# Full-width PSUM evacuation of key and query units in the first attention, 512-byte placement transfers, and a new order of projections

## The chip, the cores and the metric

The kernel runs on one core of a Trainium2 chip. The metric is device microseconds of the whole kernel. Engines are named as in the profile: PE is TensorE, ACT is ScalarE, DVE is VectorE, POOL is GpSimd, SP is SyncE, which here only issues DMA transfers.

## The reference

A decoder of two layers over x of shape (8, 128, 128): per layer a self-attention, a cross-attention and a feed-forward part, each followed by a residual sum and a layer norm. The change touches the first self-attention alone:

```python
x = _layernorm(x + _L0_attn_ref(x, wq, wk, wv, wo))      # first of six such lines
...
xq = jnp.einsum('bsh,oh->bso', x, wq)                    # wq, wk, wv: (1024, 128)
xk = jnp.einsum('bsh,oh->bso', x, wk)
xv = jnp.einsum('bsh,oh->bso', x, wv)
xq = xq.reshape(bsz, 16, seqlen, 64)                     # a reshape, not a transpose
...
scores = softmax(jnp.einsum('bhid,bhjd->bhij', xq, xk) * 64 ** -0.5)
out = jnp.einsum('bhij,bhjd->bhid', scores, xv)
```

Since the reshape does not transpose, a head is made of eight tokens, and each token gives sixteen rows of 64 numbers to it. So what a projection puts out has to be laid out anew before a head's scores can be computed.

## The kernel before, in words

**Pairs, quads, ticks.** The eight batches are worked on as four pairs (256 tokens each, p = 0 to 3). A pair has 32 heads, and four heads make a quad, so a pair has 8 quads (QP) and the attention 32 (NQ). The main loop has one tick for each quad t. In tick t PE computes the key-side scores of quad t (`scores_k`, L574 to L576), then the values of quad t - 1 (`weigh`, L592), then the query-side scores of quad t + 5 (`scores_q`, L560 and L561), which DVE reduces to row maxima (`maxima`, L1101). So the first query-side scores of pair 1, quad 8, are due in tick 3, those of pair 2 in tick 11 and those of pair 3 in tick 19.

**Projections.** A pair's projections are twelve units: 0 to 3 keys, 4 to 7 queries, 8 to 11 values. Pair 0's are done before the ticks, at eight PSUM banks; those of pairs 1 to 3 between the other work, in up to three places of a tick, at two banks in turn (`projected_at`), so that a unit waits until the bank of the last unit but one is free (`pj_free`). A table `PJ` gave the units of each tick: 3, 2, 2, 2, 1, 1, 1, 0 and again from the start for the next pair.

**Emptying a unit.** The scores are computed with float16 halves: ACT writes the upper half of a key or query unit (`empty_projection`, L899), DVE subtracts it from PSUM and writes the lower half (`lower_parts`, L1096). Both write straight into the layout that the matmuls read, in two instructions of 64 partitions, since partitions 0 to 63 and 64 to 127 of a unit belong to different columns of it. The upper half goes to partitions 0 to 63 and the lower to 64 to 127 of `KA` (keys) or `QS` (queries). `KB` is `KA` with its halves swapped, and two transfers of 64 partitions by 8 KB (SP, L330 and L332) make it. `KA`, `KB` and `QS` exist twice, for even and odd pairs.

**SP's queue.** SP issues in program order, and each wait holds back all that is behind it: all loads of inputs first; then for each pair p the two `KB` transfers, two stores of values to DRAM (L335), and, once these have landed, sixteen loads of them into `V` (L342). `scores_q` waits for `qk_in`, which these `KB` transfers raise. The order is written by hand.

**Other names of the change.** `w_abs` (L1362, L1364, L849, L1368): sums of the last feed-forward's weights, in ticks 0 to 2. `VE`: buffers of the second attention's values, which POOL sets to zero early (L431). Groups of batches in the later stages ("mid", "late") start in tick 14.

## Time and profile before

| | us |
|---|---|
| median of 3 runs (lowest to highest) | 331.54 (330.96 to 332.50) |
| the profiled execution's own time | 331.54 |
| its span in the profile | 329.7 |
| PE busy, share of the span | 253.7, 77% |
| DVE busy | 209.2, 63% |
| ACT busy | 147.6, 45% |

The profile is of one execution. Times are microseconds from the start of the span. A matmul's end is modelled, so a busy PE is not a PE at its peak; PEclk is the share of TensorE's full clock that was granted. DMA share is the mean busy share of the 16 DMA engines. In a timeline row the bracket gives how long the engine had been idle and what released it.

### The profile page before, as it was taken

Reading aid. Unit: us, or ns where it says so; the run is one execution under the profiler, and the core shown is the slowest. Engines: PE = TensorE matmul, PEld = TensorE weight load, DVE = VectorE, ACT = ScalarE, POOL = GpSimd, SP = SyncE. Lnnn points to the kernel's source line nnn. Section 1 sums busy time; section 2 is a strip of 40 time slices with the busy share of each in tenths; the row PEclk is TensorE's granted clock in tenths of the full one; section 3 lists DMA queues with packets and bytes.
Section 4 is the critical chain, followed back from the end, with each engine's and each line's share of the span. In section 5 each row is a group of like instructions: output and inputs, shape, how many; then the busy total and the mean of one; then the engine's idle time right before and its main releaser. Section 6 shows DMA issues by size and latency. Waiting matters only on the chain.

```text
span 329.7 us, 6843 instructions
## 1 busy us (share of the span) xinstructions
PE 253.7 (77%) x2658; PEld 191.9 (58%) x2658; DVE 209.2 (63%) x534; ACT 147.6 (45%) x275; POOL 72.1 (22%) x107
## 2 busy tenths in 40 slices
PE   3578679989998999798967999999887767652430
PEld 3546667978787988686844666666564434240110
DVE  2855996499657995765544666567475756354662
ACT  5962663376339545425322444453344543202651
POOL 5793000000011001443017473252020002021002
PEclk9967999999999999999978999999999896555555
DMA  7994631543142503444000800013000000000011
GB/s 233 393 258 141 139 67 66 137 104 82 67 129 64 129 34 118 103 115 51 2 1 2 155 2 2 2 40 66 3 0 2 1 2 0 0 0 1 0 32 32
DMA packets 27823, 22.86 MB, mean 69 GB/s; under 512 B 19152, under 2 KB 24400, under 8 KB 27088
## 3 DMA queue, kind: packets, MB, share of 16 engines
q1 hardware_dynamic: 27792, 22.43, 25.9%
q8 instruction: 21, 0.34, 0.5%
q14 instruction: 10, 0.08, 0.1%
HBM read 12.20 MB, written 6.03 MB: 55 GB/s over the span
## 4 chain that ended last, share of the span: by engine, by line
PE 47%; DVE 26%; ACT 13%; issue 8%; POOL 3%; DMA 1%; SPq 1%; ACTq 0%; DVEq 0%; POOLq 0%
DVE arena L1096 6%; ACT arena L899 4%; PE PS L516 4%; PE PS L619 3%; PE PS L696 3%; ACT xt L922 3%; PE PS L592 3%; PE PS L718 2%; PE PS L560 2%; PE PS L611 2%; PE PS L702 2%; PE PS L701 2%; PE PS L561 2%; POOL rstd L443 2%; DVE stats L1155 2%
## 5 line engine op out<-in xcount | busy, mean ns | idle before, releaser
L441 POOL TENSOR_SCALAR shift<-mv 128x3 f32<-128x3 f32 (+2 forms) x15 | 3.6, 241 | 233.3 <-DVE mv L1158 233.3
L1096 DVE TENSOR_TENSOR arena<-PS,arena 64x512 f16<-64x512 f32 x64 | 44.1, 690 | 9.2 <-ACT arena L899 8.0
L899 ACT ACTIVATE arena<-PS 64x512 f16<-64x512 f32 x64 | 37.8, 591 | 25.4 <-PE PS L547 24.9
L978 ACT ACTIVATE PT<-PS 128x512 f32<-128x512 f32 x32 | 19.1, 596 | 35.1 <-PE PS L702 34.9
L922 ACT ACTIVATE xt<-res,shift,rstd 128x128 f32<-128x128 f32 x42 | 17.7, 483 | 32.6 <-POOL shift L444 32.5
L1231 DVE TENSOR_REDUCE rowmax<-PS 128x4 f32<-128x512 f32 x32 | 21.9, 686 | 13.1 <-PE PS L704 12.6
L545 PE MATMUL PS<-xh,w0l 128*128 128x256 f32 x64 | 21.0, 329 | 11.8 <-DVE arena L1096 6.2
L912 ACT ACTIVATE PT<-PS 128x512 f32<-128x512 f32 x32 | 19.1, 598 | 15.8 <-PE PS L576 14.5
L1101 DVE TENSOR_REDUCE rowmax<-PS 128x4 f32<-128x512 f32 x32 | 21.7, 682 | 6.5 <-PE PS L561 6.4
L592 PE MATMUL PS<-V,PT 128*64 128x68 f32 x512 | 22.2, 229 | 1.9 <-DVE On L1125 1.9
L574 PE MATMUL PS<-arena 128*128 128x128 f16 x128 | 23.3, 221 | 0.1
L576 PE MATMUL PS<-MR,En 128*128 128x128 f16 x128 | 23.1, 219 | 0.0
L575 PE MATMUL PS<-arena 128*128 128x128 f16 x128 | 23.1, 219 | 0.0
L592 PEld LDWEIGHTS PS<-V,PT 128*64 128x64 f32 x512 | 17.8, 136 | 7.3 <-issue 2.6
L560 PE MATMUL PS<-arena 128*128 128x128 f16 x128 | 19.1, 231 | 3.5 <-issue 3.0
L545 PEld LDWEIGHTS PS<-xh,w0l 128*128 128x128 f32 x64 | 12.8, 199 | 13.6 <-DVE arena L1096 7.7
L561 PE MATMUL PS<-arena 128*128 128x128 f16 x128 | 19.0, 230 | 0.0
L546 PE MATMUL PS<-xl,w0h 128*128 128x256 f32 x64 | 18.6, 290 | 0.0
L702 PE MATMUL PS<-MR,En 128*128 128x128 f16 x128 | 18.5, 225 | 0.0
L547 PE MATMUL PS<-xh,w0h 128*128 128x256 f32 x64 | 18.5, 289 | 0.0
L905 ACT ACTIVATE VN<-PS 128x512 f32<-128x512 f32 x16 | 9.4, 596 | 18.5 <-PE PS L539 18.5
L619 PE MATMUL PS<-wo,OT 128*128 128x128 f32 x128 | 16.1, 279 | 0.1
(209 smaller groups left out, 657.0 us busy)
## 6 DMA issues: line engine op xcount, KB each, us to landing
arena<-arena SPq DMA_DIRECT2D x8, 512.0 KB, 4.9
v_piece<-VN SPq DMA_DIRECT2D x8, 512.0 KB, 2.9
V<-v_piece SPq DMA_DIRECT2D x64, 64.0 KB, 2.5
arena<-k_piece SPq DMA_DIRECT2D x4, 192.0 KB, 4.3
arena<-q_piece SPq DMA_DIRECT2D x4, 192.0 KB, 6.4
q_piece<-VN SPq DMA_DIRECT2D x6, 96.0 KB, 1.7
w<-wk SPq DMA_DIRECT2D x2, 256.0 KB, 3.4
w<-wq SPq DMA_DIRECT2D x2, 256.0 KB, 4.5
```

The source lines that it names most:

```text
L545: mm(dst, w0l[:, w, g], xh[:, x], start=True, stop=False)
L560: mm(dst, head(QS[p % 2], n), head(KB[p % 2], n), start=True, stop=False)
L561: m = mm(dst, head(QS[p % 2], n), head(KA[p % 2], n), start=False, stop=True)
L574: mm(dst, head(KB[p % 2], n), head(QS[p % 2], n), start=True, stop=False)
L575: mm(dst, head(KA[p % 2], n), head(QS[p % 2], n), start=False, stop=False)
L576: m = mm(dst, En[:, n % H, :], MR[:, b % 2, :], start=False, stop=True)
L592: m = mm(bank(4)[h * 64:h * 64 + 64, first:first + VN_COLS], PT[:, Q % SLOTS_PT, n * P + a * 64:n * P + a * 64 + 64], V[:, p % 2, 4 * q + ...
L619: m = mm(bank(5)[:, 0:P], OT[:, b % 2, g, :], wo[:, g, :], start=(g == 0), stop=(g == G - 1))
L702: m = mm(part_, En[:, n, :], MR[:, b % 2, :], start=False, stop=(h == 3))
L899: m = fn(dst[:, a], src[a * 64:(a + 1) * 64], ACT.Copy)
L922: fn(xt[:, b, :], res[:, b, :], ACT.Identity, bias=shift[:, b:b + 1], scale=rstd[:, b:b + 1]).then_inc(s(f"xn{g}"), 1)
L1096: m = tt(lower[:, a], src[a * 64:(a + 1) * 64], upper[:, a], ALU.subtract)
```

## The change

- Key and query units leave PSUM at full width: one ACT and one DVE instruction of 128 partitions by 512 for a unit, in place of two of 64 partitions each. They write into two buffers (`NAT`, parts 6 and 7 of the arena, one for keys and one for queries), each with an upper and a lower half.
- From there twelve transfers a pair (`place`) fill `KA`, `KB` and `QS`: eight for the keys, four for the queries, each of 64 partitions by 8 pieces of 512 B. The first eight start when all four key units of the pair are out of PSUM, the last four when all query units are. `scores_q` of a pair waits for all twelve.
- Four heads are interleaved in a quad: the columns of a head lie 8 bytes apart in the matmuls' operands. The host orders the tokens of `x_T` so.
- The value stores become eight transfers a pair.
- ACT empties a pair's first key unit only when the pair before has been placed. SP waits, from pair 2 on, for the scores of the pair before the last.
- The projections follow a new table `UNITS`: 3, 3, 2, 2, 2, 1, 2, 2, 2, 1, ..., 1 units in the ticks 0 to 21.
- SP's loads are split: `wo`, `xt` and the last feed-forward's weights follow the value loads of pair 0, the other late ones follow the placement of pair 2. The weight sums move to the ticks 11 to 13. POOL clears `VE` after the ticks 20, 21 and 22, and waits for pair 3's placement first.

```diff
+COPIES = 16 * 12
...
+        NAT = [part(6), part(7)]
+        def natural(which, low):
+            return NAT[which][:, low * 2048:(low + 1) * 2048]
+        def of_unit(i, low):
+            return natural(i // 4, low).rearrange("p (q g c) -> p g q c", q=QP, g=G)[:, 2 * (i % 4):2 * (i % 4) + 2]
         def head(buf, n):
-            return buf[:, n * P:(n + 1) * P]
+            return buf.rearrange("p (q x k) -> p q k x", q=QP, k=4)[:, n // 4, n % 4]
...
-        PJ = ((0, 1, 2), (3, 4), (5, 6), (7, 8), (9,), (10,), (11,), ())
+        UNITS = (3, 3, 2, 2, 2, 1, 2, 2, 2, 1, 2, 1, 2, 1, 2, 1, 2, 1, 1, 1, 1, 1)
...
+            def place(p, which):
+                sp.wait_ge(*((pj_free[1], 6 * (p - 1) + 2 * which + 2) if p else (s("qk_lo"), 4 * which + 4)))
+                for a in range(2):
+                    from_hi, from_lo = (natural(which, low)[64 * a:64 * a + 64].rearrange("p (q c) -> p q c", q=QP)
+                                        for low in range(2))
+                    for dst, top, bottom in (((QS, from_hi, from_lo),) if which else
+                                             ((KA, from_hi, from_lo), (KB, from_lo, from_hi))):
+                        to = dst[p % 2].rearrange("p (q a c) -> p a q c", q=QP, a=2)[:, a]
+                        sp.dma_start(to[0:64], top).then_inc(qk_in[p % 2], 16)
+                        sp.dma_start(to[64:P], bottom).then_inc(qk_in[p % 2], 16)
             for p in range(NPAIR):
                 b = p % 2
-                sp.wait_ge(s("qk_hi"), 8 * p + 4)
-                sp.dma_start(KB[b][64:P, :], KA[b][0:64, :]).then_inc(qk_in[b], 16)
-                sp.wait_ge(*((pj_free[1], 6 * (p - 1) + 2) if p else (s("qk_lo"), 4)))
-                sp.dma_start(KB[b][0:64, :], KA[b][64:P, :]).then_inc(qk_in[b], 16)
+                if p >= 2:
+                    sp.wait_ge(s("sk_done"), QP * (p - 1))
+                for which in range(2):
+                    place(p, which)
+                if p == 2:
+                    load_rest()
                 for h in range(2):
...
-                    sp.dma_start(v_piece[2 * p + h].rearrange("n (t c) d -> (n t) (c d)", t=8), v_half(h))\
-                        .then_inc(s(f"v_out{h}"), 16)
+                    for q in range(4):
+                        sp.dma_start(v_piece[2 * p + h, 4 * q:4 * q + 4].rearrange("k (t c) d -> t k (c d)", t=8),
+                                     v_half(h)[32 * q:32 * q + 32]).then_inc(s(f"v_out{h}"), 16)
...
+                if p == 0:
+                    load_first()
...
                 if q == 0:
-                    pe.wait_ge(qk_in[p % 2], 32 * (p // 2 + 1))
-                    pe.wait_ge(*((pj_free[1], 6 * (p - 1) + 4) if p else (s("qk_lo"), 8)))
+                    pe.wait_ge(qk_in[p % 2], COPIES * (p // 2 + 1))
...
-                    dst = by_column((KA, QS)[i // 4][p % 2][0:64, :], i)
-                    for a in range(2):
-                        m = fn(dst[:, a], src[a * 64:(a + 1) * 64], ACT.Copy)
-                    m.then_inc(s("qk_hi"), 1)
+                    if p and i == 0:
+                        act.wait_ge(qk_in[(p - 1) % 2], COPIES * ((p - 1) // 2 + 1))
+                    fn(of_unit(i, 0), bank(at).rearrange("p (g q c) -> p g q c", g=2, q=QP), ACT.Copy)\
+                        .then_inc(s("qk_hi"), 1)
...
-                for a in range(2):
-                    m = tt(lower[:, a], src[a * 64:(a + 1) * 64], upper[:, a], ALU.subtract)
-                m.then_inc(s("qk_lo") if p == 0 else pj_free[i % 2], 1)
+                tt(of_unit(i, 1), src, of_unit(i, 0), ALU.subtract)\
+                    .then_inc(s("qk_lo") if p == 0 else pj_free[i % 2], 1)
```

Three places show how the instructions move. The first is SP's queue from the start of pair 0's placement to that of pair 1's. Before:

```order
L324 DMA decay_s<-decay 128x128
L330 DMA arena<-arena 64x4096
L332 DMA arena<-arena 64x4096
L335 DMA v_piece<-VN 128x1024 x2
L342 DMA V<-v_piece 16x16x64 x16
```

In the changed kernel (the last two of pair 0's twelve, and the first two of pair 1's; in `arena<-arena` both sides are parts of the arena):

```order
L349 DMA arena<-arena 64x8x256
L350 DMA arena<-arena 64x8x256
L363 DMA v_piece<-VN 8x4x1024 x8
L370 DMA V<-v_piece 16x16x64 x16
L319 DMA wo<-wo 128x1024
L320 DMA xt<-x_tok 128x1024
L321 DMA wgu_s<-wgu 128x1024
L322 DMA wdn_s<-wdn 128x512
L349 DMA arena<-arena 64x8x256
L350 DMA arena<-arena 64x8x256
```

Pair 1's placement stands behind the sixteen loads into V as before, and now behind four large loads as well. The second place is ACT from the end of the first projections into the ticks 0 to 2. Before:

```order
L905 ACTIVATE VN<-PS 128x512 x4
L899 ACTIVATE arena<-PS 64x2x32x8 x2
L912 ACTIVATE PT<-PS 128x512
L899 ACTIVATE arena<-PS 64x2x32x8 x6
L912 ACTIVATE PT<-PS 128x512
L899 ACTIVATE arena<-PS 64x2x32x8 x4
L912 ACTIVATE PT<-PS 128x512
```

In the changed kernel:

```order
L936 ACTIVATE VN<-PS 128x512 x4
L930 ACTIVATE arena<-PS 128x2x8x32
L943 ACTIVATE PT<-PS 128x512
L930 ACTIVATE arena<-PS 128x2x8x32 x3
L943 ACTIVATE PT<-PS 128x512
L930 ACTIVATE arena<-PS 128x2x8x32 x3
L943 ACTIVATE PT<-PS 128x512
L930 ACTIVATE arena<-PS 128x2x8x32
```

Each unit is one row's instruction now, and the exponentials (`PT<-PS`) of the ticks 0, 1 and 2 have one, three and three units between them. The third place is DVE over the same ticks, from the row maxima (`rowmax`) before tick 0. Before:

```order
L1101 TENSOR_REDUCE rowmax<-PS 128x4 x5
L1107 TENSOR_SCALAR MR<-PS 16x128
L1108 SCALAR_TENSOR_TENSOR MR<-PS,MR 16x128
L1096 TENSOR_TENSOR arena<-PS,arena 64x2x32x8 x4
L1362 TENSOR_REDUCE wabs<-wgu_s 128x1 x2
L1364 TENSOR_REDUCE wabs<-wdn_s 128x1
L1096 TENSOR_TENSOR arena<-PS,arena 64x2x32x8 x2
L1101 TENSOR_REDUCE rowmax<-PS 128x4
```

In the changed kernel:

```order
L1130 TENSOR_REDUCE rowmax<-PS 128x4 x5
L1136 TENSOR_SCALAR MR<-PS 16x128
L1137 SCALAR_TENSOR_TENSOR MR<-PS,MR 16x128
L1125 TENSOR_TENSOR arena<-PS,arena 128x2x8x32 x3
L1130 TENSOR_REDUCE rowmax<-PS 128x4
```

The three units of tick 0 cost three instructions in place of six, and the three reductions over weights (`wabs`) have left the tick.

## Rows read from the trace of the kernel before

**Rows 1.** The page: busy time of each engine, share of the span, instructions.

```profile
PE 253.7 (77%) x2658; PEld 191.9 (58%) x2658; DVE 209.2 (63%) x534; ACT 147.6 (45%) x275; POOL 72.1 (22%) x107
```

**Rows 2.** The page's groups by cost: busy us, mean ns of one, idle before, releaser.

```profile
L1096 DVE TENSOR_TENSOR arena<-PS,arena 64x512 f16<-64x512 f32 x64 | 44.1, 690 | 9.2 <-ACT arena L899 8.0
L899 ACT ACTIVATE arena<-PS 64x512 f16<-64x512 f32 x64 | 37.8, 591 | 25.4 <-PE PS L547 24.9
...
L912 ACT ACTIVATE PT<-PS 128x512 f32<-128x512 f32 x32 | 19.1, 598 | 15.8 <-PE PS L576 14.5
L1101 DVE TENSOR_REDUCE rowmax<-PS 128x4 f32<-128x512 f32 x32 | 21.7, 682 | 6.5 <-PE PS L561 6.4
```

**Rows 3.** PE's waits over the whole span: us in total, times, longest.

```profile
PE PS L545 <- DVE arena L1096: 6.2, 9, 1.7
...
PE PS L537 <- DVE arena L1096: 3.8, 1, 3.8
PE PS L560 <- issue: 3.0, 1, 3.0
```

**Rows 4.** Timeline, before the ticks: start, us, engine, instruction, how many.

```profile
7.78 3.62 ACT L899 ACTIVATE arena<-PS 64x512 f16<-64x512 f32 x6
...
11.31 1.14 ACT L882 ACTIVATE w0h<-w 128x512 fp32r<-128x512 f32 x2
...
13.70 7.09 DVE L1096 TENSOR_TENSOR arena<-PS,arena 64x512 f16<-64x512 f32 x10 [0.46 <-ACT arena L899]
...
18.16 0.58 SPq L332 DMA_DIRECT2D arena<-arena  x1
```

**Rows 5.** Timeline of PE: query-side scores of quads 0, 8 and 16 start.

```profile
25.43 0.22 PE L560 MATMUL PS<-arena 128*128 128x128 f16 x1 [3.00 <-issue]
...
50.53 0.22 PE L560 MATMUL PS<-arena 128*128 128x128 f16 x1
...
83.77 0.22 PE L560 MATMUL PS<-arena 128*128 128x128 f16 x1
```

**Rows 6.** Timeline of SP: loads of pair 0's values, then pair 1's first transfer.

```profile
26.62 11.14 SPq L342 DMA_DIRECT2D V<-v_piece  x16
37.81 0.61 SPq L330 DMA_DIRECT2D arena<-arena  x1
```

**Rows 7.** Busy time by stretches (us, engines, PEclk, DMA share, GB/s): three with many projections.

```profile
30.00:50.50 20.50, 15.14 (x179) 12.97 (x179) 18.07 (x35) 12.27 (x21) 0.00 (x0) 1.00 0.43 94
64.00:82.00 18.00, 16.12 (x194) 14.20 (x193) 15.74 (x29) 11.64 (x20) 0.00 (x0) 1.00 0.43 97
98.00:121.00 23.00, 21.19 (x251) 18.92 (x249) 20.30 (x40) 15.15 (x28) 1.01 (x1) 1.00 0.32 74
```

**Rows 8.** The same view: loads; pair 0's transfers; first scores; V loads; a KB transfer.

```profile
6.00:12.00 6.00, 6.00 (x42) 6.00 (x42) 3.61 (x6) 5.39 (x11) 2.53 (x2) 1.00 1.02 405
...
25.40:28.00 2.60, 2.57 (x25) 2.32 (x26) 1.38 (x2) 0.00 (x0) 2.09 (x4) 0.53 0.42 172
36.00:38.00 2.00, 0.99 (x15) 0.77 (x13) 1.96 (x4) 1.62 (x3) 0.00 (x0) 1.00 0.44 101
73.00:73.50 0.50, 0.50 (x9) 0.49 (x8) 0.35 (x2) 0.42 (x1) 0.00 (x0) 1.00 1.26 262
...
22.00:24.00 2.00, 0.43 (x2) 0.00 (x0) 0.00 (x0) 0.60 (x1) 1.85 (x7) 0.96 0.95 197
```

**Rows 9.** Transfers of the page: how many, KB each, median us from issue to landing.

```profile
arena<-arena SPq DMA_DIRECT2D x8, 512.0 KB, 4.9
v_piece<-VN SPq DMA_DIRECT2D x8, 512.0 KB, 2.9
V<-v_piece SPq DMA_DIRECT2D x64, 64.0 KB, 2.5
...
w<-wv SPq DMA_DIRECT2D x2, 256.0 KB, 5.6
```

**Rows 10.** The chain of waits from 60 to 130 us, shares by line.

```profile
by line: DVE arena L1096 14.0%; issue 11.5%; ACT arena L899 8.7%; PE PS L619 7.2%; PE PS L611 5.4%; PE PS L592 5.3%; PE PS L560 4.2%; PE PS L561 3.3%; PE PS L574 2.7%; PE PS L545 2.6%; DVE rowmax L1101 2.6%; PE PS L576 2.6%; PE PS L575 2.6%
```

**Rows 11.** One line's instructions: ns min/median/max. Float16 operands at L560, float32r at L545.

```profile
L560 PEld LDWEIGHTS PS<-arena x128: 95/98/152, 25.4 to 144.2; 128*128 128x128 f16 x128
...
L545 PEld LDWEIGHTS PS<-xh,w0l x64: 186/189/330, 5.6 to 115.6; 128*128 128x128 f32 x64
```

More of the change, by code:

```diff
@@ L201, in decoder @@
         block = ctx.enter_context(nc.Block())
-        PJ = ((0, 1, 2), (3, 4), (5, 6), (7, 8), (9,), (10,), (11,), ())
+        UNITS = (3, 3, 2, 2, 2, 1, 2, 2, 2, 1, 2, 1, 2, 1, 2, 1, 2, 1, 1, 1, 1, 1)
         def next_projection(t, k):
-            banks = PJ[t % QP]
-            return ((t // QP + 1, banks[k]),) if t < NQ - QP and k < len(banks) else ()
+            n = UNITS[t] if t < len(UNITS) else 0
+            at = ((), (0,), (0, 2), (0, 1, 2))[n]
+            unit = sum(UNITS[:t]) + at.index(k) if k in at else None
+            return () if unit is None else ((unit // NPROJ + 1, unit % NPROJ),)
         def quad_bank(Q):
@@ new lines, in load_rest @@
+            def load_rest():
+                sp.dma_start(cT[:], ctx_T).then_inc(s("ld_ctx"), 16)
+                for dst, src in ((wx0[:, 0, :], xwq0), (wx0[:, 1, :], xwk0), (wx0[:, 2, :], xwv0),
+                                 (bx0[:, 0:1], xbq0), (bx0[:, 1:2], xbk0),
+                                 (wx1[:, 0, :], xwq1), (wx1[:, 1, :], xwq1s), (wx1[:, 2, :], xwk1),
+                                 (wx1[:, 3, :], xwk1s), (wx1[:, 4, :], xwv1),
+                                 (rot_s[:], rot)):
+                    sp.dma_start(dst, src).then_inc(s("ld_ctx"), 16)
+                for dst, src in ((bvx0[:], xbv0.partition_broadcast(P)), (wge_s[:], wge),
+                                 (bge_s[:], bge.partition_broadcast(P)),
+                                 (w1[:, 0:2, :], wqk1), (w1[:, 2, :], wv1), (b1[:], bqk1),
+                                 (bv1_s[:], bv1.partition_broadcast(P)), (wp1_s[:], wp1),
+                                 (bp1_s[:], bp1.partition_broadcast(P)), (decay_s[:], decay)):
+                    sp.dma_start(dst, src).then_inc(s("ld_mid"), 16)
@@ L430, in _, with frame_values @@
                 .then_inc(s("masks"), 1)
[L431 to L434 removed]
+            def frame_values(g):
+                if g == 0:
+                    pool.wait_ge(qk_in[1], 2 * COPIES)
+                link(pool.memset(VE[g], 0.0))
+                pool.memset(VE[g].rearrange("p (x c) -> p x c", c=32)[:, :, DH1:DH1 + 1], 1.0).then_inc(s("ve_ones"), 1)
             def rsqrt(g, k):
@@ L505, in _ @@
                     run(t, k)
+                if t in (20, 21, 22):
+                    frame_values(t - 20)
         @block.tensor
@@ L1091, in lower_parts @@
             def lower_parts(p, i):
-                src = bank(projected_at(p, i)).rearrange("p (g n t) -> p g n t", g=2, t=8)
+                src = bank(projected_at(p, i)).rearrange("p (g q c) -> p g q c", g=2, q=QP)
                 dve.wait_ge(s("qk_hi"), 8 * p + i + 1)
-                upper, lower = (by_column((KA, QS)[i // 4][p % 2][x, :], i) for x in (slice(0, 64), slice(64, P)))
-                for a in range(2):
-                    m = tt(lower[:, a], src[a * 64:(a + 1) * 64], upper[:, a], ALU.subtract)
-                m.then_inc(s("qk_lo") if p == 0 else pj_free[i % 2], 1)
+                tt(of_unit(i, 1), src, of_unit(i, 0), ALU.subtract)\
+                    .then_inc(s("qk_lo") if p == 0 else pj_free[i % 2], 1)
             def maxima(Q):
```

50 lines of the change are left out of this document (14 added, 36 removed).

## The prediction

> **What bounds the kernel now.** I read the busy times first, then the chain of waits, then the stretches between the first projections and tick 20, where the change lies. No engine is full over the whole span: PE is busy for 253.7 of 329.7 us, DVE for 209.2 [rows 1]. But in the stretches with many projections DVE nearly is: 18.07 of 20.5 us from 30 to 50.5 us, with PE at 15.14 [rows 7]. The reader is to see there that PE stands still for 20.5 - 15.1 = 5.4 us in the ticks 0 to 3, for 1.9 us in the next such stretch and 1.8 us in the third. From 60 to 130 us the chain of waits runs through DVE's lower halves for 14.0% and ACT's upper halves for 8.7%, 9.8 and 6.1 us of 70 [rows 10]. Ahead of the ticks PE waits 3.8 us for DVE to free banks, and 3.0 us for something that is no engine [rows 3]: its first scores start at 25.43 [rows 5], and the second KB transfer, issued at 18.16 [rows 4], is the only thing that they then still need. So two limits matter: the emptying of key and query units, and the transfers ahead of a pair's first scores.
>
> **Emptying.** An ACT instruction of 64 by 512 takes 591 ns and one of 128 by 512 takes 598; on DVE 690 and 682 [rows 2]. Width in partitions is free, so half of 64 instructions goes: 32 x 0.59 = 19 us of ACT and 32 x 0.69 = 22 us of DVE. Most of that stood beside PE's work. What the end can get back is what PE lost. In the ticks 0 to 3 that is 5.4 us. In the two later stretches it is at least 1.9 + 1.8 = 3.7 us, and at most half of the 15.9 us that emptying has on the chain, 8 us. I take 5 us for both, nearer to the idle rows, since the chain passes to PE as soon as DVE is quicker. The new table has no more than two units a tick after tick 1, which fits this. The weight sums leave DVE's tick 0 and arrive in the ticks 11 to 13, where a tick has one or two units: I cost the move at nothing, covered by DVE's idle time there (it now has less to do in a tick than PE), 2 us if that cover were gone. POOL's clearing takes place in the ticks 20 to 22, when POOL is nearly idle: nothing, at most some 1 us.
>
> **The transfers of a pair.** Before, 2 x 512 KB. Now 12 x 256 KB = 3.15 MB. I call their time on the DMA engines R; R is the number on which the forecast hangs. No row shows 512 B pieces within SBUF. The nearest are the KB transfers, also 64 partitions to 64 partitions: 262 GB/s at their best, and 197 GB/s while loads were still going on [rows 8]. A transfer of 512 KB lands 4.9 us after issue and one of 64 KB after 2.5 us [rows 9]: 448 KB more in 2.4 us, 191 GB/s. Small pieces do not cost much by themselves: the V loads, in pieces of 256 B, moved 101 GB/s at a share of 0.44 [rows 8], which would be 230 GB/s at a full share. So R lies between 3.15/0.262 = 12 us and 3.15/0.191 = 16.5 us; I take 14. The only row that speaks for less is the stretch of loads over 128 partitions, 405 GB/s [rows 8], R = 7.8: that is a rival. Above, the pieces are sixteen times smaller than the KB rows'. At 262 GB/s over 16 engines 512 B take 31 ns of an engine; a 256 B piece of the V loads took 16 x 256 x 0.44 / 101 = 18 ns. If the one came on top of the other, 49 ns, the 6144 pieces would take R = 19.
>
> The issue of the twelve takes 12 x 0.6 = 7 us by the KB rows [rows 4, 6] and is covered by R. Fixed time from issue to landing is about 2.4 us (the 64 KB row, [rows 9]).
>
> **Pair 0, before the ticks.** ACT starts on unit 0 at 7.78 and does three units in 3 x 0.6, to 9.6. Then come the halves of the value weights, 1.14 us [rows 4], which landed some 5.6 us [rows 9] after an issue near 4, so at 9.7. Unit 3 ends at 11.5, DVE's lower half at 12.2. The placement lands at 12.2 + 2.4 + 14 = 28.6 us; the query units are ready long before their turn. Before it was 25.4. So the first scores come 3.2 us later, though DVE is done with its sixteen halves (to 20.8, [rows 4]) six us earlier. That gain is not lost to an engine: the DMA queue gives it back.
>
> **Pair 1, due in tick 3: the step that decides.** SP's order is: placement 0, value stores, sixteen V loads, four large loads, placement 1. The stores' data queue behind placement 0 and land 1.3 us later (512 KB at 405 GB/s) at 29.9. The V loads take 11.14 us of issuing [rows 6]: 41.1. The four large loads take 2.0 us to issue; their 1.79 MB at 405 GB/s, 4.4 us, keep the engines until 41.1 + 1.8 + 4.4 = 47.3. Placement 1 moves behind them and lands at 47.3 + 14 + 0.6 = 62. In general 34 + 2R: R counts twice, and that holds for every sentence below.
> PE would be there earlier. Before, from the first scores to quad 8's took 50.53 - 25.43 = 25.1 us [rows 5]; less the 5.4 us it is 19.7, so PE arrives at 28.6 + 19.7 = 48.3 and stands for 13.7 us. Behind the waiting matmul is all of PE's program, its transposes and the next key-side scores, and behind these ACT and DVE, whose queues hold only work on what PE puts out. So the 5.4 us are hidden in the wait, and the rest is a loss: 62 - 50.5 = 11.5 us. Afterwards the granted clock is at its lower level, as it was after the wait ahead of quad 0 (0.53 in the next 2.6 us, [rows 8]); from 25.4 to 28.9 us PE went at half its pace, which cost 1.8 us. I add as much.
>
> **Pairs 2 and 3.** Pair 1's last value units come in tick 4, at about 67 us. Stored by 70, loaded by 81; then placement 2 lands at 81 + 2.4 + 14 = 97.4. Quad 16 is due 83.77 - 50.53 = 33.2 us after quad 8 [rows 5], less the gain of that stretch and with the slow clock, at 94.5. I add 3 us, with bounds of 0 (R = 12) and 8 (R = 19). Pair 3's placement stands behind 22 small loads of 0.47 us and again sixteen V loads: 89 + 10.4, 102 + 11.2, landing near 130; quad 24 is due near 131. Nothing, at R = 14.
>
> **The sum.** +11.5 (pair 1 late; pair 0's 3.2 us and the 5.4 us gained are in it) + 1.8 (clock) - 5 (later ticks) + 3 (pair 2) = +11.3. The span is 329.7 us in an execution of 331.54, which is also the median: 331.54 + 11.3 = 342.8, rounded to **343 us**.
>
> **Two rules of the pages.** The value stores now have a slowest dimension of 8. No row shows such a transfer. The Trainium skill, DMA: Bandwidth & Descriptors, "Why a DMA increments its semaphore by 16", says that a transfer goes over as many of the engines as divides that dimension, so over 8: each half's data would take 2.6 us in place of 1.3, and by it the sum is 1.3 us more.
>
> **Rivals.**
> (a) The transfers run at the loads' rate. At 405 GB/s, R = 7.8, placement 1 lands at 49.6 or, with SP's issuing, 50.5: the stall shrinks to a few us, no clock is lost, pair 2 is in time, and the 5 us later are left: 331.5 - 5 = 326.5 us, faster. The point from which it decides is 34 + 2R = 50.5 + 5, R = 10.7, or 293 GB/s. For it: loads show the rate. Against: every transfer from 64 to 64 partitions stayed at or under 262. It is also what the Trainium skill would give by DMA: Bandwidth & Descriptors, "Specifications", where 512 B is enough for line rate and the fabric's ceiling is 435 GB/s: R = 7.2. The trace disagrees with it as far as 8 KB pieces of 64 partitions go.
> (b) Near that point: R from 9.8 to 10.7 or gains and losses that cancel otherwise, 331.5 us.
> (c) The small pieces are slow: R = 19. Placement 1 lands at 72, +21.5; +1.8 - 5 + 8 = +26.3: 358 us. For it: four halves of a pair go through the same 64-partition sides at once.
> (d) The strided operand slows TensorE. 16 of 20 small matmuls of a tick read columns 8 bytes apart. If the weights then load at the 189 ns of the float32r rows and not at 98 [rows 11], each pair of instructions takes some 0.05 us more: 16 x 0.05 x 32 = 26 us, 369 us. Nothing in the rows speaks for it; no strided float16 read is there.
> (e) Full width is no gain, because writing 32-element pieces over 128 partitions takes as long as two instructions. Then the 5 us are missing, and pair 0 is later by little: 349 us.
>
> **How the numbers follow.** Forecast 0.62, (a) 0.13, (b) 0.07, (c) 0.10, (d) 0.04, (e) 0.04. The forecast's own range is 338 to 348, from R = 12 to R = 16.5. The range 330 to 356 takes in (b), (e) and part of (c), and leaves out most of (a), the rest of (c) and (d), about 0.2. A measurement of this kernel can tell about 0.5% from no change. Faster by more than that: 0.13; within: 0.07; slower: 0.80.
>
> **What the profile would show.** PE's first scores near 28.6 us, after a wait that ends with a DMA; ACT and DVE lines of 128 by 512 at 0.6 and 0.7 us, 32 each; one long wait of PE at quad 8's query-side scores, 10 to 18 us, ended by a transfer within the arena, and PEclk near 0.5 right after it; a second of 0 to 8 us at quad 16. The ticks from 12 on with almost no wait of L545 for DVE. If placement moves at over 290 GB/s the wait is gone and the forecast wrong. If PE is already waiting elsewhere in the ticks 0 to 2 (for V, whose first eight loads land at 29.9 + 5.6 + 2.5 = 38, when it is due at about 39), the stall is the same but named otherwise.

## The result, and the profile after

The changed kernel takes **367.65 us** (median of 5 runs, 365.89 to 371.79), the kernel before 331.79 beside it: a ratio of **1.107** (95% interval 1.102 to 1.112). The forecast was 343 us with a range of 330 to 356. Slower was right, the size was not. Ratios and intervals, here and below, leave out executions over 1.5% longer than the kernel's fastest, while the medians take them in; the profiles of the two runs with one operand changed are of such executions.

The page's busy times and costliest groups of the changed kernel, beside [rows 1, 2, 11], and behind them the query-side scores of the kernel before:

```profile
PE 281.3 (77%) x2658; PEld 221.5 (60%) x2658; DVE 188.1 (51%) x502; ACT 129.0 (35%) x243; POOL 72.2 (20%) x109
...
L594 PE MATMUL PS<-arena 128*128 128x128 f16 x128 | 31.6, 295 | 28.4 <-DMA arena<-arena 28.0
...
L930 ACT ACTIVATE arena<-PS 128x512 f16<-128x512 f32 x32 | 18.7, 596 | 45.2 <-PE PS L582 45.1
L594 PEld LDWEIGHTS PS<-arena 128*128 128x128 f16 x128 | 15.0, 117 | 31.0 <-issue 14.9
L1125 DVE TENSOR_TENSOR arena<-PS,arena 128x512 f16<-128x512 f32 x32 | 21.8, 690 | 20.3 <-ACT arena L930 20.3
```

```profile
L560 PE MATMUL PS<-arena 128*128 128x128 f16 x128 | 19.1, 231 | 3.5 <-issue 3.0
```

Emptying went as meant: 32 instructions of 596 and 690 ns in place of 64 each, DVE 21 us and ACT 19 us less busy. But PE is busy for 27.6 us more with the same number of matmuls, and the query-side scores (L594, L560 before) take 295 ns in the mean where they took 231. Of PE's waits (us in total, times, longest), the longest:

```profile
PE PS L594 <- DMA arena<-arena: 28.0, 3, 14.0
```

The query-side scores that end them (timeline of PE, start and us):

```profile
30.52 0.28 PE L594 MATMUL PS<-arena 128*128 128x128 f16 x1 [13.96 <-DMA arena<-arena]
...
66.32 0.29 PE L594 MATMUL PS<-arena 128*128 128x128 f16 x1 [12.31 <-DMA arena<-arena]
...
148.72 0.29 PE L594 MATMUL PS<-arena 128*128 128x128 f16 x1 [1.69 <-DMA arena<-arena]
```

These are quads 0, 8 and 24; [rows 5] had quads 0 and 8 at 25.43 and 50.53. SP's queue between them (start, us, line; three of pair 0's twelve transfers, then what leads to pair 1's first, fifth and last):

```profile
12.62 0.73 SPq L349 DMA_DIRECT2D arena<-arena  x1
...
20.55 1.50 SPq L350 DMA_DIRECT2D arena<-arena  x1
...
25.71 1.29 SPq L350 DMA_DIRECT2D arena<-arena  x1
27.05 5.94 SPq L363 DMA_DIRECT2D v_piece<-VN  x8
33.03 10.96 SPq L370 DMA_DIRECT2D V<-v_piece  x16
44.03 0.60 SPq L319 DMA_DIRECT2D wo<-wo  x1
...
46.09 0.67 SPq L349 DMA_DIRECT2D arena<-arena  x1
...
49.93 3.87 SPq L349 DMA_DIRECT2D arena<-arena  x1
...
61.17 1.20 SPq L350 DMA_DIRECT2D arena<-arena  x1
```

Once a few transfers are under way, SP spends some 1.3 us on each in place of the 0.6 of [rows 4]. 256 KB in 1.3 us are 202 GB/s, so it issues at the pace at which they are done. From the first issue to the first scores pair 0 takes 17.9 us; less the fixed 2.4 (the prediction's estimate), R = 15.5. Pair 1 takes 20.2 us, the large loads' 4.4 us ahead of it in the engines included.

Where the time is: start of the query-side scores of quads 0, 8, 16 and 24, the span, and PE's total wait for transfers within the arena, of the profiled execution of each kernel (names of the experiments are given below).

| | 0 | 8 | 16 | 24 | span | waits |
|---|---|---|---|---|---|---|
| before | 25.4 | 50.5 | 83.8 | 120.2 | 329.7 | - |
| **changed** | 30.5 | 66.3 | 105.9 | 148.7 | 367.4 | 28.0 |
| before, 8 B steps | 26.1 | 52.7 | 91.5 | 133.7 | 350.4 | - |
| before, full width | 23.7 | 44.5 | 74.5 | 108.4 | 315.6 | - |
| changed, side by side | 30.4 | 68.7 | 107.0 | 150.0 | 359.1 | 44.2 |
| changed, 4 KB pieces | 29.1 | 64.6 | 104.3 | 145.3 | 363.6 | 24.1 |
| changed, placed early | 30.4 | 60.4 | 103.4 | 147.3 | 366.2 | 24.7 |
| both of these: early, side by side | 30.4 | 59.7 | 101.1 | 145.2 | 354.2 | 39.2 |
| that, no value transfers | 30.1 | 59.1 | 95.0 | 130.3 | 340.7 | 25.1 |
| side by side, no KB | 25.2 | 57.5 | 92.1 | 130.2 | 340.2 | 25.0 |
| before, late loads | 22.2 | 44.7 | 78.1 | 114.5 | 322.0 | - |
| that, queries placed | 22.0 | 49.5 | 90.8 | 134.9 | 344.8 | 19.5 |
| that, a tick sooner | 22.2 | 50.3 | 88.4 | 128.7 | 337.2 | 13.0 |

The changed kernel loses 5.1, 10.7, 6.3 and 6.4 us in the four stretches up to quad 24, and 9.2 behind it, where nothing is placed any more but scores are still computed: this suggests two mechanisms, not one.

### The profile page after: what moved, and what is told of

It is laid out like the page before. It is cut to its first block, busy times and chain, and to the rows that moved or that the text cites. A ratio compares the mean times of both kernels' runs of the same rounds, so it can differ in the third digit from the quotient of the medians.

```text
span 367.4 us, 6833 instructions
## 1 busy us (share of the span) xinstructions
PE 281.3 (77%) x2658; PEld 221.5 (60%) x2658; DVE 188.1 (51%) x502; ACT 129.0 (35%) x243; POOL 72.2 (20%) x109
## 4 chain that ended last, share of the span: by engine, by line
PE 39%; SPq 25%; DVE 15%; ACT 7%; issue 5%; DMA 5%; POOL 3%; ACTq 0%; DVEq 0%; POOLq 0%
SPq L349 8%; SPq L350 7%; SPq L370 5%; DMA arena<-arena 4%; PE PS L551 3%; PE PS L730 3%; SPq L363 2%; ACT xt L953 2%; PE PS L594 2%; PE PS L752 2%; PE PS L626 2%; PE PS L608 2%; PE PS L595 2%; PE PS L609 2%; PE PS L736 2%
## 5 line engine op out<-in xcount | busy, mean ns | idle before, releaser
L594 PE MATMUL PS<-arena 128*128 128x128 f16 x128 | 31.6, 295 | 28.4 <-DMA arena<-arena 28.0
L609 PE MATMUL PS<-arena 128*128 128x128 f16 x128 | 37.6, 297 | 0.0
L608 PE MATMUL PS<-arena 128*128 128x128 f16 x128 | 36.1, 282 | 0.0
L930 ACT ACTIVATE arena<-PS 128x512 f16<-128x512 f32 x32 | 18.7, 596 | 45.2 <-PE PS L582 45.1
L594 PEld LDWEIGHTS PS<-arena 128*128 128x128 f16 x128 | 15.0, 117 | 31.0 <-issue 14.9
L1125 DVE TENSOR_TENSOR arena<-PS,arena 128x512 f16<-128x512 f32 x32 | 21.8, 690 | 20.3 <-ACT arena L930 20.3
L595 PE MATMUL PS<-arena 128*128 128x128 f16 x128 | 32.0, 298 | 0.0
L1009 ACT ACTIVATE PT<-PS 128x512 f32<-128x512 f32 x32 | 19.1, 595 | 35.6 <-PE PS L736 35.5
L610 PE MATMUL PS<-MR,En 128*128 128x128 f16 x128 | 31.0, 242 | 0.0
L943 ACT ACTIVATE PT<-PS 128x512 f32<-128x512 f32 x32 | 19.1, 597 | 31.5 <-PE PS L610 31.5
L1260 DVE TENSOR_REDUCE rowmax<-PS 128x4 f32<-128x512 f32 x32 | 21.9, 688 | 13.5 <-PE PS L738 13.0
L581 PE MATMUL PS<-xl,w0h 128*128 128x256 f32 x64 | 19.1, 298 | 0.0
L736 PE MATMUL PS<-MR,En 128*128 128x128 f16 x128 | 18.5, 225 | 0.0
L608 PEld LDWEIGHTS PS<-arena 128*128 128x128 f16 x128 | 15.0, 117 | 3.9 <-issue 2.9
```

The costliest lines, as they stand in the source:

```text
L594: mm(dst, head(QS[p % 2], n), head(KB[p % 2], n), start=True, stop=False)
L595: m = mm(dst, head(QS[p % 2], n), head(KA[p % 2], n), start=False, stop=True)
L608: mm(dst, head(KB[p % 2], n), head(QS[p % 2], n), start=True, stop=False)
L609: mm(dst, head(KA[p % 2], n), head(QS[p % 2], n), start=False, stop=False)
L610: m = mm(dst, En[:, n % H, :], MR[:, b % 2, :], start=False, stop=True)
L736: m = mm(part_, En[:, n, :], MR[:, b % 2, :], start=False, stop=(h == 3))
```

## Experiments: the matmuls' operands

Theory S: the columns 8 bytes apart slow the score matmuls, and this is what the forecast missed. First, undone in the changed kernel.

```diff
-            return buf.rearrange("p (q x k) -> p q k x", q=QP, k=4)[:, n // 4, n % 4]
+            return buf[:, n * P:(n + 1) * P]
```

> The changed kernel, with one edit: in the score matmuls a head is 128 columns side by side again, not 128 columns 8 bytes apart. The outputs are wrong for that, since the operands are still written interleaved; the count, the sizes and the order of all instructions and transfers are the same. In the trace of the changed kernel the matmuls of L594 and L608 start 0.11 to 0.12 us apart, where before 0.056 us. Theory S (the step of 8 bytes slows them): they go back to 0.056, which takes 0.48 + 0.51 us off each tick; the 28 ticks behind quad 8's wait give that to the end, the first ones hide it in the wait: 367.7 - 27 = 341 us, 338 to 345. Rival D (the transfers within SBUF, three times as many bytes as before, slow the matmuls' reads): the spacing stays at 0.11 and the time at 365 to 369.

Measured: 361.37 us, ratio to the kernel before 1.093 (1.086 to 1.100), 6.3 us less than the changed kernel and 20 more than expected. Its query-side scores (ns min/median/max) and PE's wait for placement:

```profile
L594 PEld LDWEIGHTS PS<-arena x128: 95/98/151, 30.4 to 175.5; 128*128 128x128 f16 x128
L594 PE MATMUL PS<-arena x128: 219/219/314, 30.4 to 175.6; 128*128 128x128 f16 x128
```

```profile
PE PS L594 <- DMA arena<-arena: 44.2, 4, 17.6
```

The matmuls are back at 219 ns. But PE now waits 44.2 us for placement in place of 28.0: most of the gain turned into waiting. The table shows where. Behind quad 24 the rest of the kernel takes 209.1 us, as before the change (209.5) and not 218.7; but quad 24 itself comes no sooner (150.0, with 148.7 in the changed kernel; its placement of pair 1 was issued 1.6 us later). So up to quad 24 the placements are so late that quicker matmuls gain nothing. The mechanism is there, and what it costs can't be read from this kernel, in which another limit stands behind it. The kernel before has none, so there the same was put in alone (the diff above reversed; it mixes heads, so its outputs are other numbers).

> The kernel before, with the one edit that its score matmuls read a head's columns 8 bytes apart (outputs wrong for that, since they are written side by side). Nothing else of the change is in it: two transfers a pair, two instructions a unit. Theory S: 32 ticks x 1.0 us = 32 us on top of 331.8, less what the ticks 0 to 3, 8 to 11 and 16 to 19 hide in their waits for DVE, some 5: 356 to 364 us. Rival D: 331 to 333 us.

Measured: 350.89 us, 1.058 (1.054 to 1.063), +19 us, less than the 356 to 364 expected. The number of transfers is that of the kernel before, so a rival by which the transfers slow the matmuls' reads is out. Two further runs of the changed kernel take the step from one operand alone, in both kinds of scores: a view `plain` (side by side) for the third argument of `mm`, the moving one, and then for the second, the weights.

```diff
-                    mm(dst, head(QS[p % 2], n), head(KB[p % 2], n), start=True, stop=False)
+                    mm(dst, head(QS[p % 2], n), plain(KB[p % 2], n), start=True, stop=False)
```

> As the first, but only the moving operand of the score matmuls is side by side; the weights are still read at a step of 8 bytes (outputs wrong for that). Theory M (the moving operand's step costs): as with both, about 341 us. Theory W (the weights' load costs): no change, 365 to 369 us. Both at once: between, 350 to 360.

> The mirror of the second: only the weights of the score matmuls are side by side, the moving operand is read at a step of 8 bytes (outputs wrong for that). Theory M: 365 to 369 us, with matmuls 0.11 us apart. Theory W: about 341 us.

Measured: 364.59 (1.090, 1.082 to 1.097) with the moving operand side by side, 367.75 (1.107, 1.100 to 1.114) with the weights. One line's instructions (ns min/median/max), of the first and then of the second:

```profile
L598 PEld LDWEIGHTS PS<-arena x128: 111/113/152, 30.5 to 176.9; 128*128 128x128 f16 x128
L598 PE MATMUL PS<-arena x128: 219/219/314, 30.5 to 176.9; 128*128 128x128 f16 x128
```

```profile
L598 PEld LDWEIGHTS PS<-arena x128: 95/115/136, 30.5 to 181.6; 128*128 128x128 f16 x128
L598 PE MATMUL PS<-arena x128: 274/294/296, 30.6 to 181.7; 128*128 128x128 f16 x128
```

It is the moving operand alone: without its step the ratio is 1.090, as without both (1.093), and without the weights' step it is 1.107, as in the changed kernel. With the moving operand side by side, the weights' step lengthens their load from 98 to 113 ns, and that hides. Last, the size of the step, 4 and 16 bytes in the kernel before, of which this is the first (the second has `q=QP // 2, k=8`; heads are mixed in both):

```diff
-            return buf[:, n * P:(n + 1) * P]
+            return buf.rearrange("p (q x k) -> p q k x", q=2 * QP, k=2)[:, n // 2, n % 2]
```

> The kernel before, with two heads interleaved in place of none: a head's columns lie 4 bytes apart in both operands of the score matmuls (the products mix heads, so the outputs are not the reference's). With 8 bytes apart the same kernel came to 350.9 us and the score matmuls to one in 0.117 us in place of 0.056. Theory T (a matmul's moving operand is fetched in lines of a fixed width, and a step is free while a line still holds enough columns): at 4 bytes the matmuls stay at one in 0.056 us and the time at 331 to 333 us. Rival U (the time grows in proportion to the step): one matmul in 0.07 to 0.09 us, 336 to 342 us. Rival V (any step costs the same): one in 0.117 us, 351 us.

> The kernel before with a head's columns 16 bytes apart in both operands of the score matmuls (the products mix heads, so the outputs are not the reference's). 4 bytes apart cost nothing (331.8 us, one matmul in 0.056 us), 8 bytes apart doubled the matmul (0.117 us, 350.9 us). Theory (bytes fetched set the time): 16 bytes double it again, one in 0.22 to 0.23 us, 390 us (380 to 400). Rival (one column a fetch is the floor, reached at 8 bytes): 0.117 us, 351 us.

Measured: 331.80 us with 4 bytes, 1.000 (0.996 to 1.005); 413.53 with 16, 1.239 (1.232 to 1.247), more than the 390 expected. Consecutive score matmuls (start, us), first of the kernel before, then with steps of 4, 8 and 16 bytes:

```profile
56.29 0.22 PE L561 MATMUL PS<-arena 128*128 128x128 f16 x1
56.34 0.22 PE L560 MATMUL PS<-arena 128*128 128x128 f16 x1
56.40 0.22 PE L561 MATMUL PS<-arena 128*128 128x128 f16 x1
```

```profile
57.62 0.22 PE L560 MATMUL PS<-arena 128*128 128x128 f16 x1
57.68 0.22 PE L561 MATMUL PS<-arena 128*128 128x128 f16 x1
57.74 0.22 PE L560 MATMUL PS<-arena 128*128 128x128 f16 x1
```

```profile
60.58 0.30 PE L561 MATMUL PS<-arena 128*128 128x128 f16 x1
60.70 0.30 PE L560 MATMUL PS<-arena 128*128 128x128 f16 x1
60.82 0.30 PE L561 MATMUL PS<-arena 128*128 128x128 f16 x1
```

```profile
90.06 0.41 PE L560 MATMUL PS<-arena 128*128 128x128 f16 x1
90.29 0.41 PE L561 MATMUL PS<-arena 128*128 128x128 f16 x1
90.53 0.41 PE L560 MATMUL PS<-arena 128*128 128x128 f16 x1
```

One in 0.06, 0.06, 0.12 and 0.23 us: free at 4 bytes, and from 8 to 16 in proportion to the bytes passed over. At 8 bytes the 16 matmuls of a tick take by this 16 x 0.061 = 1.0 us more, 31 us of PE in 32 ticks (an estimate); 19 of them reach the end. Some 6 us went into time in which PE had stood still (12.1 us of it from the first to the last query-side scores before, 6.0 with the step); where the other 6 went was not traced.

## Experiments: the placement

Theory Q: what is left is the placement's time, and SP's queue around it. Four edits of the changed kernel. The first copies pieces of 4 KB in place of 512 B, so that the columns are not those that the matmuls should read:

```diff
-                        to = dst[p % 2].rearrange("p (q a c) -> p a q c", q=QP, a=2)[:, a]
+                        to = dst[p % 2][:, 2048 * a:2048 * a + 2048]
```

> The changed kernel with the same twelve transfers a pair, of the same bytes between the same halves, but each row one piece of 4 KB and not eight of 512 B (outputs wrong for that: the columns land elsewhere). In the changed kernel a pair's pieces take 15.2 us on the DMA engines. If the small pieces cost something of their own, they go at the 262 GB/s of the transfers before, 12 us: 3 us less ahead of quad 0 and twice that at quad 8, 361 us in all (358 to 364). If only the 64-partition halves limit them, 15 us and 366 to 369.

Measured: 363.57 us, 1.096 (1.090 to 1.101). First scores at 29.1 in place of 30.5, though SP starts 0.2 us later: the small pieces cost 1.6 us in 15.5. What makes R is that both sides have 64 partitions. The rows are of pair 0's placement in the changed kernel, of the same with 4 KB pieces, and of a KB transfer in the kernel with full width alone (below), which has pieces of 4 KB too, but over 128 partitions (columns as in [rows 7], the last is GB/s):

```profile
15.00:28.00 13.00, 1.57 (x7) 0.94 (x6) 0.00 (x0) 1.95 (x4) 7.22 (x10) 0.68 0.92 206
```

```profile
15.00:26.00 11.00, 2.06 (x10) 1.36 (x8) 0.68 (x1) 2.70 (x5) 7.44 (x10) 0.81 0.98 227
```

```profile
38.00:39.00 1.00, 1.00 (x17) 1.00 (x16) 0.78 (x3) 0.72 (x2) 0.00 (x0) 1.00 0.99 406
```

The second issues pair 1's twelve between the two halves of pair 0's value loads:

```diff
-                for which in range(2):
-                    place(p, which)
+                if p != 1:
+                    for which in range(2):
+                        place(p, which)
...
+                    if p == 0 and h == 1:
+                        for which in range(2):
+                            place(1, which)
```

> The changed kernel with one move in SP's order: pair 1's twelve transfers stand ahead of the loads of pair 0's second half of V and ahead of the four large loads, not behind them. In the changed kernel they are issued from 46.1 us on and quad 8's scores start at 66.3. Theory (SP's order makes them late): they can start when pair 1's keys are out, near 42, the DMA engines then have no large loads ahead, and quad 8 starts at 58 to 60: 367.7 - 7 = 361 us (358 to 363), unless the V loads that are now behind cost a new wait at quad 4. Rival (the rate alone matters and the order is hidden): 366 to 369.

Measured: 366.09 us, 1.105 (1.099 to 1.111), no difference that counts, as the rival said. In the table quad 8 is 5.9 us earlier, quad 16 only 2.5, quad 24 1.4: each later pair loses some of it, since its own placement starts only 1.5 us (pair 2) and 1.2 us (pair 3) sooner. With the operands side by side as well:

> Both edits: score matmuls on side-by-side columns (outputs wrong for that) and pair 1's transfers early. Side-by-side columns alone gave 361.4, with PE waiting 44.2 us in all for placements in place of 28.0. If the placements are the limit once the matmuls are quick, the whole gain of the move shows: 361.4 - 8 = 353 us (350 to 356). If something else holds the later pairs, 358 to 362.

Measured: 356.06 us, 1.074 (1.069 to 1.079). PE still waits 39.2 us in four places. Which part of SP's work sets the pace of pairs 2 and 3? From this kernel the value stores and loads of the pairs 1 to 3 were taken, and all pairs read pair 0's values:

```diff
+                if p:
+                    continue
                 for h in range(2):
```

> The changed kernel with side-by-side columns and pair 1's placement ahead of the second half of pair 0's value loads and of the large loads (356.1 us), and without the value stores and value loads of the pairs 1 to 3; all pairs read pair 0's values (the outputs are not the reference's). Theory (SP's cycle of placement, stores and loads, 41 to 43 us a pair, is what makes the pairs 2 and 3 late): the waits ahead of the quads 16 and 24 go, 11 to 17 us: 341 us, 336 to 346. Rival (the placement's own transfers, or the units that they wait for, make them late): 352 us or more.

Measured: 341.34 us, 1.026 (1.017 to 1.035), as the theory said. The waits ahead of quads 16 and 24 fell from 8.35 and 8.25 us to 2.67 and nothing. The run takes away SP's issuing and the data of these transfers at once, so it does not tell the two apart. SP's queue in the changed kernel from pair 2's placement to pair 3's:

```profile
86.86 0.65 SPq L349 DMA_DIRECT2D arena<-arena  x1
...
101.95 0.64 SPq L326 DMA_DIRECT2D cT<-ctx_T  x1
...
114.23 5.50 SPq L363 DMA_DIRECT2D v_piece<-VN  x8
119.83 10.37 SPq L370 DMA_DIRECT2D V<-v_piece  x16
130.30 0.66 SPq L349 DMA_DIRECT2D arena<-arena  x1
```

Issuing the twelve takes SP 15.1 us, the 22 small loads 12.3, stores and loads of values 16.1: a round of 43 us, without a wait. The round before it, 41 us, has no small loads, but a wait of 6.9 us for value units, which PE projects only behind its own wait at quad 8. Both are longer than the 33 and 36 us in which PE did a pair before. And from the side-by-side kernel the four transfers into KB were taken, the matmuls reading KA in its place:

```diff
-                                             ((KA, from_hi, from_lo), (KB, from_lo, from_hi))):
+                                             ((KA, from_hi, from_lo),)):
```

> The changed kernel with side-by-side columns (361.4 us), and without the four transfers a pair that fill KB: eight are left of twelve, and the matmuls read KA in KB's place (the outputs are not the reference's). A pair's placement takes 10 us in place of 15. Theory (the placement's time counts, twice up to quad 8 and once for each later pair): first scores 5 us earlier, quad 8 about 9 to 10 us earlier, the later pairs keep some of it: 350 us, 346 to 354. Rival (SP's other work, the value stores and loads, sets the pace of the pairs): pair 0's 5 us alone, 356 us or more.

Measured: 342.79 us, 1.031 (1.022 to 1.040), 18.6 less than with twelve and 7 less than expected. The quads 0, 8, 16 and 24 come 5.3, 11.2, 14.9 and 19.9 us sooner. A third of R is 5 us, and it counts twice up to quad 8 and once more for each later pair: the prediction's "34 + 2R" went on to 4R by the end.

## Experiments: what emptying is worth, and a better kernel

In the kernel before, full width alone (written straight into the operand buffers, nothing laid out anew):

```diff
-                    dst = by_column((KA, QS)[i // 4][p % 2][0:64, :], i)
-                    for a in range(2):
-                        m = fn(dst[:, a], src[a * 64:(a + 1) * 64], ACT.Copy)
-                    m.then_inc(s("qk_hi"), 1)
+                    fn((KA, QS)[i // 4][p % 2][:, 512 * (i % 4):512 * (i % 4) + 512], bank(at), ACT.Copy)\
+                        .then_inc(s("qk_hi"), 1)
```

> The kernel before, with one part of the change: key and query units leave PSUM at full width, one ACT and one DVE instruction of 128 partitions each in place of two of 64. They write straight into KA and QS, side by side, the upper half into columns 0 to 2047 and the lower into 2048 to 4095, and the two KB transfers are of 128 partitions by 4 KB each. Nothing is laid out anew, so the outputs are not the reference's. It prices the gain that the forecast gave to the emptying: 5.4 us in the ticks 0 to 3 and 5 us later, in all 321 us (318 to 325). If the emptying lies beside other work (PE's own work is the bound): 328 us or more.

Measured: 317.62 us, 0.958 (0.952 to 0.964). DVE's part is changed likewise, and the two KB transfers are of 128 partitions here, which may have a share in it. The prize was 14 us; by the table 1.7 before the first scores, 4.3 up to quad 8, 3.3 and 2.5 in the next stretches, 2.3 behind.

In the kernel before, only the loads that are not needed early moved, four large ones behind pair 1's KB transfers and the others behind pair 2's, with the weight sums in the ticks 5 to 7 (the changed kernel's `load_first` and `load_rest`, called at `p == 1` and `p == 2`):

> The kernel before with two parts of the change that don't touch the layout: the loads not needed at once are issued later (four large ones behind pair 1's KB transfers, the others behind pair 2's), and the weight sums move from the ticks 0, 1, 2 to 5, 6, 7, where DVE has no unit to empty. Theory: pair 0's KB transfers no longer stand behind 34 loads in SP's order and in the DMA queue, so quad 0's scores start when the value projections are done, near 22.5 and not at 25.4, and tick 0 is 2 us shorter: 331.8 - 5 = 327 us (325 to 329). Rival: the 3 us are hidden in another wait of the ticks 0 to 3: 330 to 332.

Measured: **324.21 us, 0.978 (0.974 to 0.983)**, the fastest complete kernel here. Its first KB transfers:

```profile
13.93 0.56 SPq L334 DMA_DIRECT2D arena<-arena  x1
15.36 0.48 SPq L336 DMA_DIRECT2D arena<-arena  x1
```

The second is issued at 15.36 and not at 18.16 [rows 4], and PE no longer stands still ahead of the first scores. By the table 3.2 us of the gain come from there, 2.6 from the stretch up to quad 8 and 2.0 from behind quad 24. Can the prize be added? On top of it, the query units of pairs 1 to 3 were emptied at full width and placed by four transfers a pair, with two heads interleaved (4 bytes, pieces of 256 B):

```diff
+                if p:
+                    sp.wait_ge(pj_free[1], 6 * (p - 1) + 4)
+                    for a in range(2):
+                        to = QS[b].rearrange("p (q a c) -> p a q c", q=2 * QP, a=2)[:, a]
+                        for low in range(2):
+                            sp.dma_start(to[64 * low:64 * low + 64],
+                                         part(6)[64 * a:64 * a + 64, 2048 * low:2048 * low + 2048].rearrange("p (q c) -> p q c", q=2 * QP))\
+                                .then_inc(qk_in[b], 16)
```

> The kernel before with its late loads behind pair 1's and pair 2's transfers (324.2 us), and of the change only what fits beside the work: the query units of the pairs 1 to 3 leave PSUM at full width and are placed by four transfers a pair; keys, and all of pair 0, go the old way; two heads are interleaved (4 bytes). 12 of 32 units are emptied in one instruction. Full width in all 32 units alone brought 14.0 us, so 12 of 32 would bring 5.3 us: theory 319 us (316 to 322), without a wait of PE at the quads 8, 16 and 24. Rival (the four transfers come too late for quad 8, whose queries leave PSUM only some 6 us ahead of it): a wait of PE for a transfer at those quads of 2 to 5 us each, 326 to 335 us.

Measured: 346.78 us, 1.042 (1.039 to 1.046), worse than either expectation. The table gives a pair's last query unit in the tick in which it is first used, so that the whole placement lies bare three times. Two runs, this kernel and the one without placement, with units 5 and 7 a tick sooner:

```diff
-        PJ = ((0, 1, 2), (3, 4), (5, 6), (7, 8), (9,), (10,), (11,), ())
+        PJ = ((0, 1, 2), (3, 4, 5), (6, 7), (8,), (9,), (10,), (11,), ())
```

> The kernel with only the query units of the pairs 1 to 3 placed by transfers (346.8 us, PE waiting 19.5 us for transfers at the quads 8, 16 and 24), with one more change: the table of the projections gives the units 5 and 7 a tick sooner, so that a pair's last query unit comes in the tick before its first use and not in the same one. Theory (the four transfers lay bare because their data came too late): the last query unit leaves PSUM at about 38 us, its transfers take some 8 us, quad 8 is due at 45: waits of 2 to 3.5 us each in place of 7, 330 us (325 to 335). Rival (the transfers are slow because they share the queue with other transfers, not late): the waits stay at 5 to 7 us, 342 us or more.

> The kernel before with its late loads behind pair 1's and pair 2's transfers (324.2 us), and the same table of projections as in the run beside it: units 5 and 7 a tick sooner, nothing placed. It tells what the table does by itself. Theory: nothing, 324 us (322 to 327), since the units only come sooner. Rival (tick 1 then has three units and 12 instructions of 0.6 to 0.7 us on ACT and DVE, so that PE waits for banks): 1 to 2 us a pair more, 328 us or more.

Measured: 338.27 us, 1.024 (1.017 to 1.030), and 325.89, 0.985 (0.982 to 0.989), for the table alone. With placement PE waits 13.0 us for transfers in place of 19.5 (the row of the slower kernel, then of this one, then where this one's end):

```profile
PE PS L586 <- DMA arena<-arena: 19.5, 3, 7.2
```

```profile
PE PS L586 <- DMA arena<-arena: 13.0, 3, 7.2
```

```profile
50.33 0.29 PE L586 MATMUL PS<-arena 128*128 128x128 f16 x1 [7.20 <-DMA arena<-arena]
...
88.36 0.28 PE L586 MATMUL PS<-arena 128*128 128x128 f16 x1 [3.11 <-DMA arena<-arena]
...
128.74 0.23 PE L586 MATMUL PS<-arena 128*128 128x128 f16 x1 [2.71 <-DMA arena<-arena]
```

Quads 16 and 24 went as the theory said (3.1 and 2.7 us, from 6.6 and 5.8); quad 8 did not (7.2 before and after), its four transfers are issued at 40 us still. The account nearly closes: +13.0 of waits; +5.0 behind them, since from quad 8 to 9, 16 to 17 and 24 to 25 PE takes 4.4, 4.2 and 4.2 us in place of 2.6 each time; -5.3 for 12 of 32 units, by their share of the 14 us, an estimate. That is +12.7; the medians differ by 12.4 and the spans of the profiles, from which the waits are, by 13.5. With four transfers a pair placement still costs more than it brings.

Last, the whole changed kernel with two heads interleaved, which has free matmuls and 256 B pieces:

> The changed kernel, whole, but with two heads interleaved in place of four: the columns of a head lie 4 bytes apart, and the placement's pieces are of 256 B in place of 512 B (and the value stores four a pair in place of eight). Theory: the score matmuls go back to one in 0.056 us, which with side-by-side columns gave 367.7 to 361.4 us; if the pieces of 256 B move at the rate of those of 512 B, 361 us (358 to 364). Rival (a piece has a price of its own, as the 1.4 us between 512 B and 4 KB pieces hint): twice as many pieces make a pair's placement 17 us or more in place of 15, and it counts twice by quad 8: 366 us or more.

Measured: 372.71 us, 1.119 (1.113 to 1.124): the rival, and 11 us more than with side-by-side columns and pieces of 512 B. That the smaller pieces alone cause it is not shown, since the value stores differ too.

## Why the prediction was wrong, point by point

- **Emptying, 5.4 us in ticks 0 to 3 and 5 later.** Mechanism right; alone it brings 14.0 us where the two terms were 10.4. In the changed kernel the part up to quad 8 is hidden in the wait, as the text said.
- **R = 14.** 15.5 by pair 0, inside 12 to 16.5. Rival (a), the loads' 405 GB/s, is out, and with it (b); so is (c), R = 19. The loads' rate is real, but for transfers over 128 partitions (406 GB/s), and these have 64.
- **Pair 0, first scores at 28.6.** 30.5: R's 1.5 us and SP's start at 12.62.
- **Pair 1, "34 + 2R", quad 8 at 62.** 66.3. With R = 15.5 the formula gives 65; the rest is the value stores, which take 5.94 us to issue, so that the value loads start at 33.03 and not at 29.9. The wait is 12.3 us where 13.7 was forecast: PE came later, too, since its matmuls were slower (with side-by-side columns it needs 20.8 us from the first scores, where the text had 19.7).
- **Clock, 1.8 us.** Right in kind: from quad 8 to quad 9 it takes 5.5 us, and 3.5 in the kernel before with the same steps. The stretch after the wait ran at the lower level of the clock, 0.50 (columns as in [rows 7]):

```profile
66.30:68.90 2.60, 2.58 (x14) 1.98 (x15) 0.69 (x1) 0.05 (x1) 0.00 (x0) 0.50 0.24 98
```

- **Pairs 2 and 3, +3: the first step that failed.** The text had "The issue of the twelve takes 12 x 0.6 = 7 us" and is "covered by R". SP took 15.1 us, the pace of the data, 8 us more, and everything behind it in the queue was late by as much, pair after pair; the value stores took SP 5.5 us where the text gave them some 3, and pair 2's placement started 5.9 us late already. So quad 24, due near 131 and to be placed by 130, came at 148.7, and at 150.0 with side-by-side columns. The waits themselves were 0 and 1.7 us, nearly right as numbers, but only because PE was slow itself: with quick matmuls they were 5.5 and 7.5. With the columns side by side the kernel still takes 361.4 us, so 18 of the 25 us by which the forecast fell short do not need the step: 6.7 by quad 8 (68.7 against 62), 12 more by quad 24 (150.0 against 131), nothing behind it.
- **Rival (d), chance 0.04: the second step that failed.** The strided operand did slow TensorE. The text said that nothing in the rows spoke for it, which is no evidence against: no row had such an operand, and the term stood at nothing, without bounds, in the sum. Undone in this kernel it is worth 6.3 us; alone it costs 19. That the rival's 369 us came near the result is luck: it was put on the weights' load, which costs nothing, and without the late placements the moving operand's step would not have brought the time there.
- **Rival (e)**, full width no gain, is out by 596 and 690 ns.

The sum in the terms that were measured alone: -14.1 (emptying, by the spans) + 19.1 (step of 8 bytes) = +5.0, which of the 35.9 us leaves **+30.9** for placement, its queue and the slow clock, as a remainder. The moved loads and weight sums, which the forecast put at nothing, bring 7.7 alone; if that holds here too, the remainder is 38.6. These do not add: with the step undone the time falls by 6.3 us, not by 19, with four transfers of twelve left out as well by 25.

## What to carry to other kernels

Count what a layout asks of both sides: an instruction saved where PSUM is emptied can come back as bytes to copy within SBUF (here 3.1 MB a pair at some 200 GB/s) and as steps in a matmul's moving operand, and a term for which the trace has no row belongs into the sum with bounds, not among the long shots. Where transfers of one queue serve stage after stage, compare the queue's work for a stage with the engines' time for it; if it is longer, an engine's gain turns into waiting, and what helps is work taken out of the queue, or data ready a stage ahead. SP's issue of a transfer cannot be taken from a row in which few are under way: here it went from 0.6 us to the 1.3 us that the data took. An effect that hides behind another limit is priced in the kernel without that limit.

## What was not expected of the hardware

- A float16 moving operand of 128 by 128 costs 0.056 us with its columns 2 or 4 bytes apart, 0.117 with 8 and 0.233 with 16; as weights the same columns cost nothing that shows. The Trainium skill, SBUF — State Buffer, "Specifications (TRN2)", wants two hits in each line of 16 bytes for full bandwidth, by which a step of 8 bytes would be free; the runs don't agree, and they decide.
- The strided matmuls do not follow the clock. Right behind the wait, at a granted clock of 0.50, they come as they do at full clock, one in 0.12 us (with 16 bytes one in 0.23 at both; side by side one in 0.107 at 0.50 and in 0.056 at 1.00), so that the step costs next to nothing there:

```profile
66.42 0.30 PE L595 MATMUL PS<-arena 128*128 128x128 f16 x1
66.54 0.30 PE L594 MATMUL PS<-arena 128*128 128x128 f16 x1
66.66 0.30 PE L595 MATMUL PS<-arena 128*128 128x128 f16 x1
```

- Transfers from 64 partitions to 64 within SBUF moved at 206 GB/s with pieces of 512 B and at 227 with 4 KB; from 128 to 128 with 4 KB at 406. SP's issue of one of 256 KB then stretches from 0.6 to 1.3 us.
